# A language-model tower on one core: the row minimum of two score tiles in one VectorE instruction, and VectorE's side work moved ahead of it

## The reference

```python
embedded = emb_table[src]                                # block 1: a gather, then
h = embedded @ W_e2h + b_e2h                             # six gated convolutions
conved = _conv1d_same(x, conv_w[i], conv_b[i])
a, g = jnp.split(conved, 2, axis=1)
x = (a * jax.nn.sigmoid(g) + x) * SCALE

attn1 = softmax(q1 @ k1.T * scale)                       # block 2: two attentions, 8 heads of 16 columns
attn2 = softmax(q2 @ k2.T * scale)
gate_in = concat(window_stats(attn1), window_stats(attn2))   # mean, std, max and min of each row of attn,
alpha = sigmoid(relu(relu(gate_in @ gw1 + gb1) @ gw2 + gb2) @ gw3 + gb3)   # averaged over windows of 4 rows
fused = alpha * attn1 + (1 - alpha) * attn2              # then fused @ v, @ Wo

y = gelu(x_attn @ fc1_w[e] + fc1_b[e]) @ fc2_w[e]        # block 3: an expert for each stretch of tokens
out = gelu(y @ next_w.T + next_b)
```

## Time and profile before

| what | value |
|---|---|
| median of three runs | 5982.09 us |
| the profiled execution's own time | 5978.36 us |
| its span, from the first to the last instruction | 5975.9 us |
| TensorE busy (matmuls) | 5203.4 us, 87% |
| VectorE busy | 5115.8 us, 86% |
| ScalarE busy | 5221.3 us, 87% |
| POOL busy | 2454.1 us, 41% |
| mean granted clock of TensorE | 0.955 of full speed |

### The profile page before, as it was taken

How to read it: one execution, slowest core, us unless ns; L and a number is a source line. 1 busy time by engine, 2 the same in 40 slices (tenths; PEclk the granted TensorE clock), 3 DMA queues, 4 the chain that set the end, 5 groups by cost and what they waited for, 6 DMA issues and landing times.

```text
span 5975.9 us, 121038 instructions
## 1 busy us (share of the span) xinstructions
PE 5203.4 (87%) x34070; PEld 2503.5 (42%) x34070; DVE 5115.8 (86%) x7715; ACT 5221.3 (87%) x7937; POOL 2454.1 (41%) x4439
## 2 busy tenths in 40 slices
PE   6988989889898988989889898988889899898985
PEld 4443434444343443434334343443434344343443
DVE  2989899898998989899898988989899898988982
ACT  2999989899898989989889898989989899898984
POOL 6525344252433525344352433525344352533423
PEclk8999999999999999999999999999999999999997
DMA  1001010010101001010010101001010010101000
GB/s 37 20 23 27 17 31 20 21 27 23 27 19 29 20 21 27 19 31 19 21 28 23 27 19 29 20 21 27 20 31 18 22 28 21 27 20 29 19 22 12
DMA packets 164933, 140.87 MB, mean 24 GB/s; under 512 B 89196, under 2 KB 108268, under 8 KB 164140
## 3 DMA queue, kind: packets, MB, share of 16 engines
q1 hardware_dynamic: 159100, 124.09, 9.0%
q0 software_dynamic: 4352, 8.92, 0.7%
q10 hardware_dynamic: 816, 0.02, 0.0%
HBM read 21.26 MB, written 8.91 MB: 5 GB/s over the span
## 4 chain that ended last, share of the span: by engine, by line
PE 44%; issue 18%; DVE 15%; ACT 11%; POOL 8%; SPq 1%; DMA 1%; DVEq 1%; ACTq 1%; POOLq 1%
PE ps_w L389 19%; PE ps_t L389 10%; PE ps_o L389 9%; DVE neg_s L715 7%; PE ps_s L389 6%; DVE rowmin L723 4%; ACT exps L586 3%; ACT junk L579 3%; DVE bn L735 1%; SPq L330 1%; DVE o_raw L731 1%; POOL part L866 1%; POOL ctmp L986 1%; POOL ctmp L998 1%; ACT hpre L635 1%
## 5 line engine op out<-in xcount | busy, mean ns | idle before, releaser
L715 DVE TENSOR_SCALAR_CACHE_REDUCE neg_s<-ps_s 128x1024 f32<-128x1024 f32 x2048 | 2487.5, 1215 | 599.3 <-PE ps_s L389 526.2
L723 DVE TENSOR_REDUCE rowmin<-neg_s 128x1 f32<-128x1024 f32 x2049 | 2489.5, 1215 | 0.0
L579 ACT ACTIVATE junk<-neg_s,negmax 128x1024 bf16<-128x1024 f32 x2048 | 2353.0, 1149 | 149.4 <-DVE neg_s L715 145.1
L586 ACT ACTIVATE exps<-ps_t 128x1024 f32<-128x1024 f32 x2060 | 2110.6, 1025 | 255.6 <-PE ps_t L389 252.7
L389 PE MATMUL ps_t<-qst,kst 99*128 99x512 bf16 x4120 | 1293.3, 397 | 367.5 <-ACT exps L586 364.1
L389 PE MATMUL ps_o<-exps,v_cur 128*32 128x256 f32 x16512 | 1360.8, 402 | 272.6 <-DVE o_raw L731 240.7
L389 PE MATMUL ps_s<-kst,qst 96*128 96x512 bf16 x4096 | 1260.4, 389 | 44.1 <-DMA kst<-part 35.8
L389 PE MATMUL ps_w<-xc,cw 128*128 128x256 f32 x4704 | 1185.3, 388 | 1.0
L389 PEld LDWEIGHTS ps_w<-xc,cw 128*128 128x128 f32 x4704 | 914.7, 195 | 223.3 <-ACT chan L590 8.9
L389 PEld LDWEIGHTS ps_o<-exps,v_cur 128*32 128x32 f32 x16512 | 330.1, 109 | 1198.1 <-issue 643.9
L866 POOL TENSOR_SCALAR ctmp<-ug 128x256 f32<-128x256 f32 x408 | 165.8, 406 | 1554.7 <-ACT ug L655 1533.0
(11 more groups left out here) (181 smaller groups left out, 4025.1 us busy)
## 6 DMA issues: line engine op xcount, KB each, us to landing
qst<-part SPq DMA_DIRECT2D x1542, 32.0 KB, 2.0
kst<-part SPq DMA_DIRECT2D x1542, 32.0 KB, 2.0
qst<-mrow SPq DMA_DIRECT2D x1028, 1.5 KB
out_dram<-z SPq DMA_DIRECT2D x17, 512.0 KB, 3.2
fc1s<-in_fc_w SPq DMA_DIRECT2D x17, 256.0 KB
fc2s<-in_fc_w SPq DMA_DIRECT2D x17, 256.0 KB
cw<-in_conv_w SPq DMA_DIRECT2D x1, 2304.0 KB
odif<-in_table,idx POOLq DMA_INDIRECT x136
```

Of the source, the lines that this page charges most:

```text
L579: nc.scalar.activation(junk[:, n % 2, :], neg_s[:, n % SLOTS_S, :], ACT.Exp, scale=-1.0, bias=negmax[:, r, t:t + 1], accum_out=sumsq[:, r, ...
L586: nc.scalar.activation(exps[:, n % RING, :], ps_t[:, :, :].rearrange("p c q -> p (c q)"), ACT.Exp, scale=0.5).then_inc(s_exp, 1)
L715: nc.vector.tensor_scalar(neg_s[:, n % SLOTS_S, :], ps_s[:, n % 2, :], -1.0, None, ALU.mult, ALU.min, accum_out=negmax[:, r, t:t + 1]).the ...
L723: nc.vector.tensor_reduce(rowmin[:, r, t:t + 1], neg_s[:, m % SLOTS_S, :], axis=AX, op=ALU.max, negate=True).then_inc(s_min, 1)
```

## The change

`row_min` is called in even steps alone. It takes tiles n-2 and n-1 in one instruction, from two neighbouring slots of `neg_s` into two columns of `rowmin`, and adds 2 to its counter. It stands behind the side tasks of its step, which so follow `row_max` directly, in odd steps too. In even steps `row_max` waits in addition until the minimum that still reads its slot is done, and POOL's wait before the statistics counts three more.

```diff
--- before.py
+++ after.py
@@ -711,17 +711,19 @@
                     wait_side(dve, "body", i, "pool", ("unit", n // T - 2) if n // T > 1 else None)
                 dve.wait_ge(s_scores, i * STEPS + n + 1)
                 dve.wait_ge(s_sq, i * STEPS + n + 1)
+                if n % 2 == 0:
+                    dve.wait_ge(s_min, i * STEPS + n + 2)
 
                 nc.vector.tensor_scalar(neg_s[:, n % SLOTS_S, :], ps_s[:, n % 2, :], -1.0, None, ALU.mult, ALU.min,
                                         accum_out=negmax[:, r, t:t + 1]).then_inc(s_max, 1)
 
             def row_min(i, n):
 
-                m = (n - 1) % STEPS
-                r, t = m // T % RING, m % T
+                m = (n - 2) % STEPS
+                r, t, s = m // T % RING, m % T, m % SLOTS_S
                 dve.wait_ge(s_max, i * STEPS + n + 2)
-                nc.vector.tensor_reduce(rowmin[:, r, t:t + 1], neg_s[:, m % SLOTS_S, :], axis=AX, op=ALU.max,
-                                        negate=True).then_inc(s_min, 1)
+                nc.vector.tensor_reduce(rowmin[:, r, t:t + 2], neg_s[:, s:s + 2, :], axis=AX, op=ALU.max,
+                                        negate=True).then_inc(s_min, 2)
 
             def collect(phase, i, j):
 
@@ -827,6 +829,7 @@
             last.then_inc(s_init, 1)
             dve.sem_inc(s_out, 16)
             dve.sem_inc(s_max, 2)
+            dve.sem_inc(s_min, 2)
             dve.wait_ge(s_load, 16 * N_LOADS)
             dve.wait_ge(s_init, 4)
             for tk in PRE:
@@ -838,9 +841,10 @@
                     pos.update(n=0)
                     for n in range(STEPS):
                         row_max(i, n)
-                        row_min(i, n)
                         for tk in STEP[n]:
                             task("body", i, tk)
+                        if n % 2 == 0:
+                            row_min(i, n)
             assert pos["n"] == pos["per"], pos
             row_min(NB, 0)
             pos.update(n=0)
@@ -873,7 +877,7 @@
                 u = (j - 2) % U
                 r = u % RING
                 pool.wait_ge(s_sq, i * STEPS + max(T * (j - 1), 0) + SLOTS_S)
-                pool.wait_ge(s_min, i * STEPS + max(T * (j - 1), 0) + 1)
+                pool.wait_ge(s_min, i * STEPS + max(T * (j - 1), 0) + 4)
                 if j == 2:
                     wait_side(pool, phase, i, "act", ("snap",))
                 tt(dif_all[:, u, :], rowmin[:, r, :], negmax[:, r, :], ALU.add)
```

## The result

The changed kernel takes 6070.4 us (median of 4 runs, 6066.7 to 6073.3) where the kernel before, run beside it, takes 5980.4: a ratio of 1.015 (95% interval 1.0133 to 1.0168), 90 us slower. The forecast was 6045 us in a range from 5945 to 6110. The profiled execution has a span of 6069.6 us.

The account below looks back on a forecast made before the run. No engine was taken as the bound throughout. Per pass 2.2 + 1.2 + 1.0 + 0.8 + 0.8 - 1.35 - 0.7 = 3.95 us, 63 us over 16 passes, hence 6045 us; range 5945 to 6110.

Parts of the forecast that it names:

- the rival with a fixed part of 0.15 us: Each pair saves 0.15 us, not 0.06, and half of the 64 lie on the path: 5999 us; chance 0.08.
- Its worth on the path: Pairs where VectorE is the bound, mainly steps 104 to 127: 12 pairs save 0.7 us a pass.
- Step 120: The pair runs behind `mrow`, which starts unchanged after POOL's split; the maximum of step 121 comes later: +2.2 us a pass.
- Step 8: The pair behind a late `mrow` delays the next maximum and `squares(9)`: +1.2 us a pass (0 to 2.2).
- Step 48: The pair behind `mrow` and moments delays `squares(49)`, which already waits 1.75 us: +1.0 us a pass (0 to 1.3).
- Step 16: The pair behind `snap` makes `squares(17)` wait 1.07 us longer; TensorE slightly ahead afterwards: +0.8 us a pass (0 to 1.2).
- The step that failed: Where TensorE is the bound, the next scores come behind the same matmuls, covering VectorE's delay; with `snap` at +0.8.
- `wo`, `h2e`, `ln1`, `v`: Tasks in even steps 40, 106, 108, 124, less gains of odd neighbours: +0.8 us a pass together (0 to 3.2).
- The transposes: Units in steps 61, 69 and 77 start transposes earlier for TensorE: 1.35 us a pass gained (0 to 1.9).
- The waits: Signs: VectorE's wait before `mrow` up to about 73 us, ScalarE's for maxima up some 50, TensorE's for transposes down 20 or more.
- The rival in which ScalarE swallows the late maxima: ScalarE lags enough to swallow late odd maxima and later `mrow`, above all at steps 121 and 9: 5930 us; chance 0.16.
- the one in which gains and losses cancel: Steps 8, 16 absorbed, `wo`, `h2e`, `ln1`, `v` free, pairs save 1.9 us a pass: 0 a pass, 5982 us; chance 0.11.

Follow-up runs that it names:

- e9: The kernel after with the pair's one instruction split into two single-tile minima, one behind the other in the same place: 6075.6 us.
- e5: The kernel after with the pair ahead of the side tasks in steps 8 and 120 alone: 6033.6 us.
- e1: The kernel after with the pair straight behind the maximum, ahead of all side tasks, in even steps: 5967.7 us.
- e11: e1 with the units' transposes ahead of the maximum in odd steps, except in step 21: 5943.5 us.
- e3: The kernel before, single minima kept, with the side tasks moved ahead of the minimum in odd steps alone: 5897.4 us.
- e10: The kernel after with the pair ahead of the side tasks in steps 8, 16, 24 and 120: 5994.9 us.
- e12: The kernel before with the unit's transposes ahead of the minimum in steps 61, 69 and 77 alone: 5957.5 us.
- e4: The kernel after with 14 unread matmuls more per pass, filling TensorE's gaps in steps 23, 50 and 51: 6060.6 us.
- e7: The kernel after with six unread matmuls more per pass, ahead of scores_t in step 23 alone: 6060.2 us.

## Why the prediction came out as it did

- **The instruction.** Predicted 2283 ns and 2.20 us from start to start; the group L725 has 2272 ns, and 979 pairs with a maximum straight behind them are followed by it 2.19 us later. Right, and so the rival with a fixed part of 0.15 us falls. The Trainium skill, "Vector Engine (DVE) Microarchitecture Reference", section "5.2 Measured stream behaviour on trn2", states 1.0417 ns per column and about 75 ns per instruction where instructions follow each other. The trace agrees: by that, an estimate, a pair takes 2.21 us and saves 0.075, and the starts show 2.19 and 2 x 1.13 - 2.19 = 0.07.
- **Its worth on the path.** Predicted 0.7 us per pass, 11 us; e9 gives 7, within the noise of the two kernels, so nothing speaks against it and nothing shows it.
- **Step 120.** Predicted +2.2 with `mrow` at an unchanged time. It starts 4.23 us behind the maximum and not 3.61. The maxima show +1.68 from 120 to 126; with the pair first in this step it is 2.2 us less (e5), so the value is right as the price of the order. Another 1.05 us from step 126 on was not foreseen: every kernel with the pair in even steps has it (e1 +0.96, e11 +1.09), e3 with single minima has none.
- **Step 8.** Predicted +1.2, and +1.0 in the trace from step 8 to 10. But e5 shows that most of it is swallowed by step 54, and nothing is left by step 120: too high.
- **Step 48.** Predicted +1.0; in the 10 passes in which the clock stays at 2.4 GHz there, the loss from 48 to 54 is 0.9 to 1.3 us, mostly 1.07; in the 6 in which it falls it is 2.7 to 3.8. The mean is +1.71. The term was right; the clock on top of it was not foreseen.
- **Step 16.** Predicted +0.8 because `squares(17)` would wait 1.07 longer. It does (1.52 against 0.24), but by step 22 nothing of it is left in the maxima. The lag goes on in ScalarE instead: the exponentials that `scores_t` of step 23 waits for start 4.30 us behind the maximum of step 22, 3.50 in the kernel before (pass 5 of each), and TensorE stands for 1.75 us.
- **The step that failed** is the one that put `win`, `hid1` and `hid2` in 23, 25 and 27 at no cost, "where TensorE is the bound, the next scores come behind the same matmuls, which covers it", together with `snap` at +0.8. Steps 10 to 26 lose 2.63 us per pass, 42 us, all of it behind step 22. In the 4 passes without a fall of the clock steps 22 to 26 lose 0.6 in the mean, in the others 1.7 to 3.9. About half of it hangs on the order in steps 16 and 24 (26 us by step 26 in e10); TensorE idles, and its clock falls with it. How much is the idle time and how much the clock stays open (7 to 23 us for the clock). The term is 1.8 us per pass too small, 29 us, about the 25 by which the forecast was short. That the rest came out right is partly luck: step 48, and 120 with the stretch behind it, cost 1.2 more than was forecast, step 8 and the smaller terms about as much less.
- **`wo`, `h2e`, `ln1`, `v`.** Predicted +0.8 together; the maxima show +0.60 behind step 40, -0.07 behind 106, -0.05 behind 108 and +0.19 behind 124, 0.67 in all. The odd neighbours, whose gain the term was to include, take off 0.27 (steps 38 to 40), 0.16 (102 to 104) and 0.05 (122 to 124), which leaves 0.2: too high.
- **The transposes.** -1.35 predicted for 61, 69 and 77; e12 gives 20 us, 1.26 per pass. In after steps 54 to 80 gain 1.64. Right, to the units counted. That units elsewhere would gain 0.06 alone is right for 29, 45, 93 and 109, but only because the pair stands ahead of them: their stretches gain nothing in after and 0.8 to 1.1 us each with single minima (e3). The prediction weighed the change as a whole and did not ask what its parts would do without each other.
- **The waits.** `mparts` was forecast at 73 us by 32 waits; it is 107.3 in 95 waits, about six units of a pass instead of two. ScalarE's wait was to rise by some 50 us and rose by 161.8. As forecast it stands in odd steps (285.4 of the 306.9 us), but 9, 17, 49 and 121 alone rise by 91 us, and 41, 105 and 125, which were counted small or not at all, by 65.

The rival in which ScalarE swallows the late maxima falls with `squares(121)`, which waits 2.72 us; so does the one in which gains and losses cancel. As to the parts, two errors met: the gain of the move was sized at 22 us where without the pair it is 78, and the pair's loss beside it, 70 us, was not seen.

## What to carry to other kernels

Less work on an engine is no gain where the work is bunched. Two minima in one place set back every second maximum by a full minimum, and with it the tasks that other engines wait for; here that cost 70 us beside single minima in the same order, though VectorE had 80 us less to do. When a task that may wait for another engine is moved ahead of work that can run at any time, the work loses its use as cover. A task whose inputs are there and whose result another engine waits for belongs ahead: the transposes in odd steps, `alpha` in step 32. And a change of several parts is best sized part by part before it is summed, and in more than one order, since the parts depend on each other: -78, +70 and +98 look like +90 and hide a kernel that is 78 us faster.

## What the runs showed of the hardware that was not expected

TensorE's clock fell to half, 1.2 GHz, behind one and the same wait of 1.75 us in 12 passes and stayed at 2.4 GHz in 4, with the same instructions ahead of it; where it fell, the six rows of a convolution took 2.77 us instead of 1.46, and the stretch from the maximum of step 24 to that of 26 took up to 8.1 us instead of 5.2. With matmuls in the wait (e4, e7) no half-clock time was left in steps 22 to 27 of any pass, but these matmuls held the next ones back by 0.93 us, and the kernel was only 5 to 7 us faster.
